# Products b x du and s x du of the state-space units: written to SBUF tiles instead of in place in PSUM

## What is computed

```
A = -exp(A_log)
delta, B, C = split(x @ W_dbc.T);  delta = softplus(delta * W_dt + b_dt)
h[t] = exp(delta[t] * A) * h[t-1] + (delta[t] * x[t]) * B[t]     # a scan over time
y[t] = sum_n h[t, n] * C[t, n] + Dp * x[t]
```

## Time and profile before

| what | value |
|---|---|
| median of 3 runs | 638.44 us (637.91 to 639.03) |
| the profiled execution, its own time | 639.52 us |
| its span | 637.8 us |
| PE busy | 568.4 us (89%) |
| DVE busy | 523.7 us (82%) |
| ACT busy | 513.2 us (80%) |
| POOL busy | 436.8 us (68%) |
| granted TensorE clock, mean | 0.977 |

### The profile page before, as it was taken

One profiled execution on the slowest core, in us unless ns is written; L12 is line 12 of the kernel. 1 busy time (PEld: TensorE's weight loads), 2 busy tenths in 40 slices (PEclk: granted clock), 3 DMA queues, 4 the chain that ended last, 5 costly groups with the idle time before them and its releaser, 6 DMA issues.

```text
span 637.8 us, 22844 instructions
## 1 busy us (share of the span) xinstructions
PE 568.4 (89%) x9531; PEld 299.1 (47%) x9531; DVE 523.7 (82%) x924; ACT 513.2 (80%) x1044; POOL 436.8 (68%) x597
## 2 busy tenths in 40 slices
PE   3777678899999999999899999999999999999993
PEld 2333234545454554555454455554555544545441
DVE  5898999999979898988888988989799887653442
ACT  1335658989989999998888998999989887988780
POOL 7757899788777877876776777697785866423120
PEclk9999869999999999999999999999999999999996
DMA  3432223122121322122121222121200100000001
GB/s 78 84 80 65 57 56 73 43 59 54 40 51 26 79 50 49 36 55 52 24 61 42 61 48 60 41 65 36 65 21 20 28 20 15 20 15 10 7 13 30
DMA packets 77574, 28.51 MB, mean 45 GB/s; under 512 B 69271, under 2 KB 77463, under 8 KB 77463
## 3 DMA queue, kind: packets, MB, share of 16 engines
q1 hardware_dynamic: 71290, 25.92, 17.9%
q10 hardware_dynamic: 6173, 1.05, 0.9%
HBM read 13.25 MB, written 3.05 MB: 26 GB/s over the span
## 4 chain that ended last, share of the span: by engine, by line
PE 55%; DVE 16%; ACT 14%; POOL 6%; issue 4%; ACTq 2%; DMA 1%; SPq 1%; DVEq 0%; POOLq 0%
PE ring L1283 8%; PE ring L1362 6%; PE ring L1375 6%; PE ring L1470 5%; PE ring L1269 4%; PE ring L1441 3%; PE ring L1450 3%; PE ring L1258 2%; ACT pm L1066 2%; DVE ring L1732 2%; PE ring L1238 2%; PE ring L1421 2%; PE ring L1352 2%; DVE hidw L1860 2%; ACT hid L1116 1%
## 5 line engine op out<-in xcount | busy, mean ns | idle before, releaser
L1066 ACT ACTIVATE pm<-ring 93x744 f32<-93x744 f32 x128 | 96.3, 782 | 11.0 <-PE ring L1362 10.0
L1362 PE MATMUL ring<-q_exp,qk 32*93 32x372 f32 x512 | 56.2, 507 | 7.7 <-POOL q_exp L910 1.1
L1860 DVE TENSOR_TENSOR hidw<-hid,ring 128x744 f32<-128x744 f32 x48 | 44.3, 923 | 17.9 <-PE ring L1431 13.3
L1375 PE MATMUL ring<-pm,v 97*32 97x93 f32 x2048 | 53.5, 245 | 1.3 <-DVE base_A L1736 0.6
L1109 ACT ACTIVATE hid<-ring,b_col 128x372 f32<-128x372 f32 x96 | 49.4, 568 | 4.1 <-PE ring L1450 3.0
L1375 PEld LDWEIGHTS ring<-pm,v 97*32 97x32 f32 x2048 | 41.7, 109 | 16.0 <-ACT pm L1066 3.4
L910 POOL TENSOR_TENSOR q_exp<-qk,mask_q 128x1488 f32<-128x1488 f32 x16 | 43.0, 2687 | 8.9 <-DVE qk L1790 8.9
L1116 ACT ACTIVATE hid<-ring,b_col 128x744 f32<-128x744 f32 x48 | 42.2, 879 | 7.6 <-PE ring L1441 5.7
L893 POOL TENSOR_TENSOR base_C<-base_C,carry_C 128x744 f32<-128x744 f32 x16 | 28.4, 1777 | 27.1 <-DVE carry_C L1741 19.1
L1441 PE MATMUL ring<-hid,w 64*64 64x372 f32 x384 | 40.1, 488 | 0.6 <-ACT rows_hi_D L990 0.3
L1450 PE MATMUL ring<-nrm_f,w 64*64 64x372 f32 x384 | 39.4, 485 | 0.0
(11 more groups left out here) (366 smaller groups left out, 1757.2 us busy)
## 6 DMA issues: line engine op xcount, KB each, us to landing
xin_A<-in_x_dram SPq DMA_DIRECT2D x62, 93.0 KB
xin_B<-in_x_dram SPq DMA_DIRECT2D x62, 93.0 KB
x_A<-x_A SPq DMA_DIRECT2D x32, 93.0 KB, 3.0
x_B<-x_B SPq DMA_DIRECT2D x32, 93.0 KB, 2.7
x_C<-x_C SPq DMA_DIRECT2D x32, 93.0 KB, 2.2
out_dram<-osb SPq DMA_DIRECT2D x15, 186.0 KB
x_D<-x_D SPq DMA_DIRECT2D x32, 46.5 KB, 2.3
w<-in_L_ffn_expert_w_dram SPq DMA_DIRECT2D x6, 48.0 KB
```

Source lines behind the costliest of these rows:

```text
L1066: a.activation(pm[q % 2][h][0:TOUT].rearrange("m a j n -> m a (j n)"), out_of(f"att.s{q}{h}", g)[0:TOUT, :, 0:COLS], ACT.Square, bias=2.0, ...
L1362: ins = mm(o[h][0:TOUT, b, 0:COLS], qk[r:r + 32, 1, q * TOUT:(q + 1) * TOUT], q_exp[r:r + 32, q].rearrange("p j n -> p (j n)"), start=True ...
L1375: ins = mm(o[32 * j:32 * j + 32, 0, h * TOUT:h * TOUT + TOUT], rows[:, at:at + 32], pm[q % 2][h][:, b, j, :], start=(b == 0), stop=(b == 1 ...
L1860: tt(hidw[k][:], hid2[:], out_of(f"ffn.g_{k}", g)[:, :, 0:COLS], ALU.mult).then_inc(me, 1)
```

## The change: what it does

`vin` writes b x du to `carry` and `scan` runs there in place. `base` writes s x du to the tile `base`, and `based` adds D x x there in place. The wait for POOL's `y` of the group before moves from `scan` to `vin`, that for POOL's `y` or `pooled` from `based` to `base`. In `JOBS`, the banks of b are released by `vin` and not `scan`, those of s by `base` and not `based`. The tables of all engines and the banks are written anew for this; they hold the same steps. Of 1000 entries of PE 340 stand elsewhere, by at most 6 places; of DVE's 670 entries 411, by at most 37 (`most`, a small step, moves farthest); of POOL's 293 entries 119, by at most 6; of ACT's 917 entries 430, by at most 18; of SP's 115 entries 61, by at most 11. The mean distance from `vin` to `scan` in DVE's table goes from 1.7 to 2.4 places for A and from 2.2 to 4.1 for B, that from `base` to `based` from 2.1 to 3.3 for D and from 1.5 to 2.4 for A; the others stay within one place.

```diff
@@ -235,310 +235,310 @@
...
-                    "C.base:13 C.based:13 A.base:14 ffn.hidw1:9 A.based:14 A.vin:14 A.scan:14 ffn.hn:10 att.hn:12 B.quad:15 "
...
+                    "C.based:13 A.base:14 A.based:14 ffn.hidw1:9 A.vin:14 A.scan:14 ffn.hn:10 att.hn:12 B.quad:15 A.carry:14 "
...
@@ -551,7 +551,7 @@
...
         JOBS = {f"{u}.{j}": (2, f"dve {u}.{r}") for u in UNITS
-                for j, r in (("z", "quad"), ("b", "scan"), ("s", "based"), ("c", "carry"))}
+                for j, r in (("z", "quad"), ("b", "vin"), ("s", "base"), ("c", "carry"))}
...
@@ -1721,19 +1721,19 @@
                 if s == "vin":
                     need(g, f"pe {u}.b")
                     need(g, f"pool {u}.du")
-                    tt(b_made(u, g), b_made(u, g), du[u][:], ALU.mult).then_inc(me, 1)
+                    need(g, f"pool {u}.y", back=1)
+                    tt(carry[u][:], b_made(u, g), du[u][:], ALU.mult).then_inc(me, 1)
                 if s == "scan":
                     need(g, f"dve {u}.vin", f"act {u}.decay")
-                    need(g, f"pool {u}.y", back=1)
-                    v.tensor_tensor_scan(carry[u][:], dec[u][:], b_made(u, g), 0.0, ALU.mult, ALU.add).then_inc(me, 1)
+                    v.tensor_tensor_scan(carry[u][:], dec[u][:], carry[u][:], 0.0, ALU.mult, ALU.add).then_inc(me, 1)
                 if s == "base":
                     o = made_by("s")
                     need(g, f"pool {u}.du")
-                    tt(o, o, halves(du[u][:]), ALU.mult).then_inc(me, 1)
+                    need(g, f"pool {u}.{'y' if u == 'D' else 'pooled'}", back=1)
+                    tt(halves(base[u][:]), o, halves(du[u][:]), ALU.mult).then_inc(me, 1)
                 if s == "based":
                     need(g, f"dve {u}.base")
-                    need(g, f"pool {u}.{'y' if u == 'D' else 'pooled'}", back=1)
-                    stt(halves(base[u][:]), xs[u][:, 0::2, :], d_col[:, l:l + 1], out_of(f"{u}.s", g)[:, :, 0:wide],
+                    stt(halves(base[u][:]), xs[u][:, 0::2, :], d_col[:, l:l + 1], halves(base[u][:]),
                         ALU.mult, ALU.add).then_inc(me, 1)
                 if s == "carry":
                     o = made_by("c")
```

## The result

The changed kernel takes **730.28 us** (median of 3 runs, 730.12 to 731.33) against 638.44 us before: a ratio of 1.142 (95% interval 1.140 to 1.145), 91.8 us more. The prediction said slower with 0.90, 688 us, and 654 to 735 us. The direction and the mechanism held; the size was too small by 42 us.

The account below looks back on a forecast made before the run. PE led, with DVE and POOL setting the pace from 40 to 120 us; turns would make DVE bound. DVE's 500 us at 5.4% idle gave +48, plus 2 outside: 638.4 + 50, about 688 us, range 654 to 735.

Parts of the forecast that it names:

- The path taken in turns: DVE instructions with two SBUF inputs and POOL's share one path to SBUF, each for a whole instruction; about 434 of 480 us.
- three small router instructions: Router instructions on DVE, such as L1833 and L1845, whose uneven times and ends just after POOL's were read as turns.
- Unheld speed: When not held, scan stays at 1.70 us and based at 0.99; vin and base save 1.2 us on DVE.
- The half rate: Rival: based with two SBUF sources that aren't bf16 takes about twice its 0.99 us; about 745 us, chance 0.04.
- the router's 0.8 ns an element: From L1833 and L1845: two SBUF inputs are no slower than based from PSUM, at most 1.3 ns an element.
- Banks, moved waits: Earlier bank release gains 0 to 16.5 us, nearest 4, only while PE bounds; waits moved to vin and base cost 0.
- What DVE waits: Scans and based from 40 to 520 us: 120 x 0.78 x 0.6 = 56 us behind POOL, plus 11 us for second waits.
- being passed over: One in ten scans or based isn't let in and waits for one more POOL instruction: 12 x 0.9 = 11 us.
- From waits to time: From 40 to 520 us DVE, occupied 500 us with 5.4% idle, needs 528 us for what took 480: +48.
- POOL's delay: POOL's instructions get longer beside DVE's turns; named as a sign, but given no price in the sum.
- The tables: New tables move steps by a few places; no price but the upper bounds.
- the turns at 92% use of the path: Upper end: 516.7 us of turns need 562 us, +82, or 720; with two in ten not let in, 735.

Follow-up runs that it names:

- after_pool_fills: The changed kernel with POOL's steps three, du, y, pooled and qe replaced by memsets that only write SBUF: 640.36 us.
- the filled pair: The kernel before and the changed kernel, both with POOL's steps three, du, y, pooled and qe replaced by memsets: 639.21 and 640.36 us.
- replayed: The kernel before with the DVE and POOL delays, recorded with new operands in old tables, added as fixed work: 721.88 us.

## Why the prediction was right, and where its size was off

**The path taken in turns.** Right, and read from three small router instructions of before. Scans are held like the others, which no row of before could show. The Trainium skill ("SBUF — State Buffer", section "Who interferes with whom") had said it of every DVE instruction with two SBUF inputs. after_pool_fills shows that all of the cost hangs on it.

**Unheld speed.** Right: `vin` 922 ns, scan 1.70 us, `based` 0.98. The half rate that the Trainium skill states ("Vector Engine (DVE) Microarchitecture Reference", section "Points that are easy to get wrong") isn't there for this instruction on this chip; the router's 0.8 ns an element had told so. (The sum of that rival, 688 + 57/0.946, is 748 and not 745.)

**Banks, moved waits.** The waits moved ahead cost 0.7 us for `vin` and 0.7 for `base`. Of the 0 to 16.5 us for banks nothing measurable shows where PE still bounds (the filled pair, tables and moved waits included); what they are worth in after no run separates.

**What DVE waits.** Summed 67 us, measured 71.0. Its parts were off in opposite ways, and that the total came out is in part luck: 71 held of 128, 1.0 us each, where the sum had 94 (120 x 0.78) with 0.6 us and 11 us for being passed over.

**From waits to time: the step that failed**, "500 / 0.946 = 528 us for what takes 480, so +48". It took the idle share of DVE in its fullest stretch (5.4%) for the one that would be left. From 40 to 640 us DVE was busy for 73.42 + 349.16 + 71.58 + 30.92 = 525.1 of 600 us, which leaves 12.5%. With that share the same sum gives 500 / 0.875 = 571 us, +91. So this one term holds the whole miss, and the experiments tell what it is made of. The delays come in lumps of up to 5.4 us, and DVE doesn't catch up behind them: played back alone, DVE's delays cost 62 us, more than their own 58, where even ones, 50 us of busy time, cost 41.

**POOL's delay: the part that had no term.** I wrote that POOL pays too, and used its turns for the upper bound, but the sum has only DVE. POOL became longer by 73.8 us, in the loop delta, `du`, `vin`, scan, `carry`, `y`, `pooled`; its 107 us of idle time weren't free for that. In the old tables it adds 20 us to DVE's 62.

**The tables** cost 8 us more, for which there was no price but the upper bounds. 62 + 20 + 8 = 90 us of the 91.8. Why these tables are worse is open. One difference: DVE is held there for 71 us and not 58, with a scan of 7.1 us among them; whether that lies in the order or in chance wasn't tested.

**The range.** 730 us lies 5 us below its upper end. That end came from another sum, the turns at 92% use of the path with two in ten passed over, which no run tests. That the range held is therefore partly luck.

**PE.** Its busy time grew from 568.4 to 585.4 us for the same 9531 matmuls, at a mean granted clock of 0.925 of full speed against 0.977; from 40 to 120 us, where PE works 48.8 of 80 us, it was 0.74. Part of PE's work there ran at the lower level of 1.2 GHz. The prediction left that out. It comes with the delays and not with the turns: replayed, where no scan and no `based` is held, was granted 0.924 to 0.939 in its four runs. What it is worth in us the runs don't separate.

## What to carry to other kernels

When an operand of a DVE instruction moves from PSUM to SBUF, count its SBUF tensor inputs: with two of them, the scans and `based` of these runs took turns with the GpSimd instructions that read SBUF, each for its whole length. Add up both engines' turns, charge the wait to both, and don't count on idle time: here 134 us of waits on two engines (DVE's 58 and POOL's 76, the old tables) cost 83. Where such a pair can't be avoided, a wait between GpSimd's instructions lets DVE in at each end; where it can, as with the PSUM operand here, leave it in PSUM.

## What the runs showed of the hardware that I had not expected

- A held DVE instruction is passed over only where GpSimd's next instruction has started before the end of the one ahead: 11 of 39 against 0 of 43 with a gap (78 ns the shortest), and 0 of 66 with waits put between.
- A wait for a turn can last far longer than one instruction: 5.4 us for a scan of 1.7 us.
- Uneven delay costs more than even delay: 49.8 us more of busy time evenly over 128 places on DVE cost 41 us, 56.1 us in 58 of these places, up to 4.2 us at once, cost 62.
- A router step of GpSimd that reads SBUF was longer beside DVE's new operands (`gate_rest` 444 ns against 269), while memsets in the same run kept their 720 ns.
